# Moving the transposes of the normalised rows ahead of the attention-times-values matmuls

## The chip, the cores and the metric

The kernel runs on all 8 cores of one Trainium2 chip. Each core does the same program on its own 2048 tokens (plus a window of 128 on either side). The metric is the device time in microseconds of the slowest core.

## The reference

```python
def _L0_attn_ref(x, w_qkv):            # x (2, 8192, 1024), 16 heads of 64, windows of 128
    q, k, v = jnp.split(x @ w_qkv, 3, axis=-1)
    ...                                # keys of the window before, the own one, the one after
    scores = einsum('bhnqe,bhnke->bhnqk', q * scale, k_ctx)
    scores = where(valid, scores, NEG)
    out = einsum('bhnqk,bhnke->bhnqe', softmax(scores), v_ctx)

x = layernorm(x + _L0_attn_ref(x, w_qkv))
x = layernorm(x + _L0_ffn_ref(x, ...)) # 8 experts, top 2, d_ff 4096, gelu, all experts computed
```

## The kernel before

One core works in three stages. First it computes q, k and v for its tokens. Then comes attention, window by window, with the first layernorm; its result is kept transposed in x1T. Then come the experts: 32 units, each 512 matmuls with 512 columns.

The instructions of every engine are put in an order written out by hand: helpers (MM for PE, DV for DVE, AC for ACT, SY for SP's queue) append to one list for each engine, with the semaphores that an instruction waits for. An engine works through its list in order. All matmuls have the line of a helper (L151), so they are told apart by tile.

The attention stage is one loop over 256 steps g (L616). A step is a head h of a window w. Windows go in pairs, and the steps alternate between the two windows of a pair: 32 steps a pair, 8 pairs. So an even g belongs to the first window of the pair and an odd g to the second. Iteration g issues, in this order:

- st_nm_exp(g): the row maximum of the scores on DVE (L399) and the exponential on ACT (L407). For the very first and the very last window a mask is added on DVE ahead of it (L391).
- plan_scores(g + 3): the scores matmul (ps_sc) of three steps ahead. There are three score banks, so it waits for the exponential of g.
- st_tr(g): three transposes of the probabilities on PE into one of two banks, ps_pt, by the parity of g.
- st_recip(g - 2): a reciprocal on DVE (L467).
- st_evpt(g - 1): the copy of the transposed probabilities out of ps_pt into probsT (three slots). For an even step it is on DVE (L435), so it is DVE work of the odd iterations; for an odd step it is on ACT (L430).
- st_av(g - 1): three matmuls, probabilities times values (ps_av).
- Up to three evacuations of ps_av on DVE (L477) while some are pending. After the last head of a window follow the residual sum (plan_stt, L492) and the sum of squares on ACT (L511, and L514 on DVE); the rest of the statistics (plan_tail_stats2, L520, L523, L526 on DVE, L530 and L533 on ACT) comes in a later iteration and the normalisation (plan_tail_stats3, L539 and L547 on DVE, which writes x1tmp) in a later one still. That is done by a countdown of 2 and 4 iterations in pend_work.
- The transposed result. For each window gen_tail_mm_pieces makes two pieces. A piece is four transposes of x1tmp on PE into the ps_pt bank of parity g + 1, and one DVE copy of 512 columns into x1T (L570 in the first piece, p12, L586 in the second, p34). Pieces are put in pend_tmpiece once the window is normalised, and each iteration issues at most one, at its end. Windows of the last pair get theirs after the loop.

A ps_pt bank is free for the next transposes when the copy that last read it is done, be it L435, L430, L570 or L586.

Of the kernel before, what the change touches and what calls it, by code (L numbers as in the profile page):

```python
# [85 lines left out]
def build_nc(debug=False):  # L86
# [62 lines left out]
    def MM(dst, lhsT, rhs, start, stop, waits=(), inc=None):  # L149
        fn = (lambda _d, _l, _r, _s, _e:  # L150
              lambda t: t.matmul(_d, _l, _r, start=_s, stop=_e))(dst, lhsT, rhs, start, stop)  # L151
        return p.op("tensor", fn, waits=waits, inc=inc)

    def DV(fn, waits=(), inc=None, drain=True):
        r = p.op("vector", fn, waits=waits, inc=inc)
        if drain:
            p.op("vector", lambda v: v.drain())  # L157
        return r

    def AC(fn, waits=(), inc=None):  # L160
        return p.op("scalar", fn, waits=waits, inc=inc)

    def SY(fn, waits=(), inc=None, n=16):
        w = list(waits)
        if inc is not None:
            w.append((inc, p.val[inc]))
        return p.op("sync", fn, waits=w, inc=inc, n=n)
# [179 lines left out]
    def avbank(w, h):  # L347
        return (4 * (w // 2) + (2 if h >= 8 else 0) + (w % 2)) % 3
# [24 lines left out]
    def plan_scores(g):  # L373
        w, h = steps[g]
        bi = g % 3
        scb[g] = bi
        hp, hb = h // 2, (h % 2) * 64
        w_ = list(bk_sc[bi].rw())
        if g < 2:
            w_ += [(s_ac, qkv_ac_end)]  # L380
        sc_v[g] = MM(ps_sc[bi][:],
                     q_b[hb:hb + 64, hp, 128 * w:128 * (w + 1)],
                     k_b[hb:hb + 64, hp, 128 * w:128 * w + 384],
                     start=True, stop=True, waits=w_, inc=s_mm)

    def st_nm_exp(g):
        w, h = steps[g]
        bi = scb[g]
        bp = g % 3
        if w in (0, NCH - 1):  # L390
            mv = DV((lambda _b: lambda v: v.tensor_tensor(  # L391
                out=ps_sc[_b][:], in0=ps_sc[_b][:], in1=mask_s0[:], op=ALU.add))(bi),
                waits=[(s_mm, sc_v[g]), (s_x, mask_state["v"])], inc=s_dv, drain=True)
            if w == 0 and h == H - 1:
                mask_state["reload"] = mv
        nmw = [(s_mm, sc_v[g])]
        if g - 3 in exp_v:
            nmw.append((s_ac, exp_v[g - 3]))
        nmv = DV((lambda _bi, _bp: lambda v: v.reduce_max(out=stc(C_NM + _bp), in_=ps_sc[_bi][:],  # L399
                                                          axis=AX.X, negate=True))(bi, bp),  # L400
                 waits=nmw, inc=s_dv, drain=False)
        ew = [(s_dv, nmv)]
        if g - 3 in tr_v:
            ew.append((s_mm, tr_v[g - 3]))
        if (w - 2, h) in recip_v:
            ew.append((s_dv, recip_v[(w - 2, h)]))
        exp_v[g] = AC((lambda _bi, _bp, _s: lambda s: s.activation(  # L407
            out=probs_u[:, _bp, :], in_=ps_sc[_bi][:], func=AF.Exp,
            bias=stc(C_NM + _bp), scale=1.0, accum_out=stc(C_L + _s)))(bi, bp, lri(w, h)),
            waits=ew, inc=s_ac)  # L410
        bk_sc[bi].release = [(s_ac, exp_v[g])]

    def st_tr(g):
        bp = g % 3
        bt = g % 2
        for c in range(3):
            w_ = [(s_ac, exp_v[g])] + (bk_pt[bt].rw() if c == 0 else [])
            tr_v[g] = MM(ps_pt[bt][:, 128 * c:128 * (c + 1)],
                         probs_u[:, bp, 128 * c:128 * (c + 1)], I_b[:],
                         start=(c == 0), stop=(c == 2), waits=w_,  # L420
                         inc=(s_mm if c == 2 else None))

    def st_evpt(g):
        bt = g % 2
        sl = g % 3
        epw = [(s_mm, tr_v[g])]
        if g - 3 in av_v:
            epw.append((s_mm, av_v[g - 3]))
        if g % 2 == 1:
            ev = AC((lambda _b, _s: lambda s: s.copy(out=probsT[:, _s, :], in_=ps_pt[_b][:, 0:384]))(bt, sl),  # L430
                    waits=epw, inc=s_ac)
            bk_pt[bt].release = [(s_ac, ev)]
            evpt_v[g] = ("ac", ev)
        else:
            ev = DV((lambda _b, _s: lambda v: v.tensor_copy(out=probsT[:, _s, :], in_=ps_pt[_b][:, 0:384]))(bt, sl),  # L435
                    waits=epw, inc=s_dv, drain=False)
            bk_pt[bt].release = [(s_dv, ev)]
            evpt_v[g] = ("dv", ev)

    def st_av(g):  # L440
        w, h = steps[g]
        sl = g % 3
        aw = avbank(w, h)
        kind, ev = evpt_v[g]
        evw = (s_ac, ev) if kind == "ac" else (s_dv, ev)
        if h % 8 == 0:
            ug = 4 * (w // 2) + (2 if h >= 8 else 0) + (w % 2) - 3
            if ug >= 0:
                tw = 2 * (ug // 4) + (ug % 2)
                th = 7 if (ug % 4) < 2 else 15  # L450
                force_drain(lambda: (tw, th) in evac_v)
        for c in range(3):
            w_ = [evw]
            if h % 8 == 0 and c == 0:
                w_ += bk_av[aw].rw()
            av_v[g] = MM(ps_av[aw][:, 64 * (h % 8):64 * (h % 8) + 64],
                         probsT[:, sl, 128 * c:128 * (c + 1)], v_b[:, w + c, 64 * h:64 * h + 64],
                         start=(h % 8 == 0 and c == 0), stop=(h % 8 == 7 and c == 2),
                         waits=w_, inc=(s_mm if c == 2 else None))
        avg_by_wh[(w, h)] = av_v[g]  # L460

    def st_recip(g):
        w, h = steps[g]
        rw_ = [(s_ac, exp_v[g])]
        if (w - 2, h) in evac_v:
            rw_.append((s_dv, evac_v[(w - 2, h)]))
        recip_v[(w, h)] = DV((lambda _s: lambda v: v.reciprocal(  # L467
            out=stc(C_RI + _s), in_=stc(C_L + _s)))(lri(w, h)),
            waits=rw_, inc=s_dv, drain=False)
# [130 lines left out]
    pend_tmpiece = []  # L600
    pend_work = []

    def force_drain(cond):
        while not cond():
            we, he = pend_evac.pop(0)
            plan_evac(we, he)
            if he == 15:
                plan_stt(we)
                plan_tail_stats1(we)
                pend_work.append([2, (lambda _w: lambda: plan_tail_stats2(_w))(we)])  # L610
                pend_work.append([4, (lambda _w: lambda: plan_tail_stats3(_w))(we)])
# [4 lines left out]
    for g in range(NST):  # L616
        w, h = steps[g]
        st_nm_exp(g)
        if g + 3 < NST:
            plan_scores(g + 3)  # L620
        st_tr(g)
        if g >= 2:
            st_recip(g - 2)
        if g >= 1:
            st_evpt(g - 1)
            st_av(g - 1)
            wp, hp_ = steps[g - 1]
            if hp_ == 7:
                pend_evac += [(wp, hh) for hh in range(8)]
            if hp_ == 15:  # L630
                pend_evac += [(wp, hh) for hh in range(8, 16)]
        if mask_state["reload"] is not None and not mask_state.get("reloaded"):
            mask_state["v"] = SY(lambda e: e.dma_start(out=mask_s0[:], in_=mrd),
                                 waits=[(s_dv, mask_state["reload"])], inc=s_x)
            mask_state["reloaded"] = True
        n_done = 0
        while pend_evac and n_done < 3:
            we, he = pend_evac[0]
            if (we, he) not in recip_v:
                break  # L640
            plan_evac(we, he)
            pend_evac.pop(0)
            n_done += 1
            if he == 15:
                plan_stt(we)
                plan_tail_stats1(we)
                pend_work.append([2, (lambda _w: lambda: plan_tail_stats2(_w))(we)])
                pend_work.append([4, (lambda _w: lambda: plan_tail_stats3(_w))(we)])
        for item in pend_work:
            item[0] -= 1  # L650
        while pend_work and pend_work[0][0] <= 0:
            pend_work.pop(0)[1]()
        if h == 0 and w % 2 == 0 and w >= 2:
            pend_tailmm += [w - 2, w - 1]
        while pend_tailmm and pend_tailmm[0] in x1ap_v:
            pend_tmpiece += gen_tail_mm_pieces(pend_tailmm.pop(0))
        if pend_tmpiece:
            pend_tmpiece.pop(0)((g + 1) % 2)
    st_evpt(NST - 1)
    st_av(NST - 1)  # L660
    wlast, hlast = steps[NST - 1]
# [332 lines left out]
```

How the kernel before makes its waits and increments, by code:

```python
            def body(eng_obj):  # L59
                for waits, fn, inc, n in self.streams[name]:
                    for (s, v) in waits:
                        eng_obj.wait_ge(s, v)
                    bi = fn(eng_obj)
                    if inc is not None:
                        bi.then_inc(inc, n)
```

## Time and profile before

| | us |
|---|---|
| median of 3 runs | 4558.41 |
| lowest run | 4555.35 |
| profiled execution | 4560.75 |
| its span (slowest core) | 4558.3 |
| span of the fastest core | 4539.9 |

The profile is of one execution, on the slowest core (core 5). PE is TensorE, PEld its weight loads, DVE VectorE, ACT ScalarE. In the timeline a row has the start in us from the start of the span, the duration in us, the engine, the line, the operation, what it writes and reads, the shapes and the count, and in brackets how long the engine had been idle ahead of it and what ended the wait. The attention stage lies between about 350 and 864 us of the span, and the experts fill the rest of it.

### The profile page before, as it was taken

Reading aid. Unit: us, or ns where it says so; the run is one execution under the profiler, and the core shown is the slowest. Engines: PE = TensorE matmul, PEld = TensorE weight load, DVE = VectorE, ACT = ScalarE, POOL = GpSimd, SP = SyncE. Lnnn points to the kernel's source line nnn. Section 1 sums busy time; section 2 is a strip of 40 time slices with the busy share of each in tenths; the row PEclk is TensorE's granted clock in tenths of the full one; section 3 lists DMA queues with packets and bytes.
Section 4 is the critical chain, followed back from the end, with each engine's and each line's share of the span. In section 5 each row is a group of like instructions: output and inputs, shape, how many; then the busy total and the mean of one; then the engine's idle time right before and its main releaser. Section 6 shows DMA issues by size and latency. Waiting matters only on the chain.

```text
span 4558.3 us, 48557 instructions; the slowest of 8 cores (4539.9 to 4558.3 us)
## 1 busy us (share of the span) xinstructions
PE 4108.2 (90%) x19776; PEld 1912.6 (42%) x19776; DVE 1141.1 (25%) x1978; ACT 902.2 (20%) x1415; POOL 76.8 (2%) x92
## 2 busy tenths in 40 slices
PE   5865555479999999999999999999999999999995
PEld 3333333234444444444444444444444444444442
DVE  1016666631111111111111111111111111111126
ACT  1224444211111111111111111111111111111111
POOL 0000000000000000000000000000000000000000
PEclk9885555579999999999999999999999999999997
DMA  6652000012222222222222222222222222222211
GB/s 115 100 86 48 19 19 19 1 19 38 38 37 37 37 38 37 37 37 38 37 38 42 43 44 39 38 37 37 37 37 38 37 37 37 38 37 38 43 32 74
DMA packets 97483, 187.26 MB, mean 41 GB/s; under 512 B 3426, under 2 KB 24290, under 8 KB 97258
## 3 DMA queue, kind: packets, MB, share of 16 engines
q0 software_dynamic: 89616, 157.36, 21.5%
q1 hardware_dynamic: 7650, 26.81, 1.7%
q8 instruction: 161, 2.64, 0.2%
q14 instruction: 56, 0.46, 0.0%
HBM read 333.12 MB, written 8.39 MB: 75 GB/s over the span
## 4 chain that ended last, share of the span: by engine, by line
PE 86%; DVE 6%; issue 3%; DMA 2%; ACT 1%; DVEq 1%; ACTq 0%; SPq 0%; POOLq 0%
PE ps_y L151 39%; PE ps_h L151 39%; PE ps_qk L151 4%; PE ps_pt L151 2%; DVE stats L399 2%; PE ps_sc L151 2%; DMA W1g<-wqkv 1%; DMA xch_q<-xh 1%; ACT probs_u L407 1%; DVEq L157 1%; DVE attn_sb L477 1%; DVE xpre L492 0%; DVE y_acc L787 0%; DVE outb L855 0%; DVE probsT L435 0%
## 5 line engine op out<-in xcount | busy, mean ns | idle before, releaser
L151 PE MATMUL ps_h<-x1T,W1g 128*128 128x512 bf16 x8192 | 1778.0, 380 | 36.0 <-ACT hpr L888 36.0
L151 PE MATMUL ps_y<-W2g,hpr 128*128 128x512 bf16 x8192 | 1783.4, 380 | 0.4 <-DVE y_acc L787 0.4
L913 DVE SCALAR_TENSOR_TENSOR y_acc<-ps_y,wgt,y_acc 128x1024 f32<-128x1024 f32 x512 | 657.1, 1283 | 2811.5 <-PE ps_y L151 2810.8
L151 PEld LDWEIGHTS ps_h<-x1T,W1g 128*128 128x128 bf16 x8192 | 802.6, 98 | 1006.0 <-issue 42.7
L151 PEld LDWEIGHTS ps_y<-W2g,hpr 128*128 128x128 bf16 x8192 | 803.2, 98 | 971.9 <-issue 12.6
L888 ACT ACTIVATE hpr<-ps_h,b1T 128x1024 bf16<-128x1024 f32 x512 | 570.4, 1114 | 2945.3 <-PE ps_h L151 2945.3
L151 PE MATMUL ps_sc<-k_b,q_b 64*128 64x384 bf16 x256 | 122.3, 480 | 217.5 <-ACT probs_u L407 214.7
L407 ACT ACTIVATE probs_u<-ps_sc,stats 128x384 bf16<-128x384 f32 x256 | 149.5, 584 | 253.6 <-DVE stats L467 245.9
L151 PE MATMUL ps_qk<-xT_S,W1g 128*128 128x512 bf16 (+3 forms) x640 | 140.3, 389 | 45.2 <-DMA W1g<-wqkv 31.2
L399 DVE TENSOR_REDUCE stats<-ps_sc 128x1 f32<-128x384 f32 x256 | 138.8, 545 | 2.9
L151 PEld LDWEIGHTS ps_sc<-k_b,q_b 64*128 64x128 bf16 x256 | 25.7, 101 | 251.2 <-issue 244.6
L151 PE MATMUL ps_pt<-I_b,probs_u 128*128 128x128 bf16 x768 | 128.5, 305 | 1.5 <-ACT probs_u L407 1.4
L151 PEld LDWEIGHTS ps_qk<-xT_S,W1g 128*128 128x128 bf16 x640 | 66.7, 110 | 117.9 <-issue 70.8
L435 DVE CAST probsT<-ps_pt 128x384 bf16<-128x384 f32 x128 | 71.1, 556 | 121.5 <-PE ps_pt L151 119.0
L151 PEld LDWEIGHTS ps_pt<-I_b,probs_u 128*128 128x128 bf16 x768 | 61.2, 125 | 85.8 <-issue 85.8
L151 PE MATMUL ps_av<-v_b,probsT 128*128 128x64 bf16 x768 | 93.9, 248 | 0.7 <-ACT probsT L430 0.6
L151 PEld LDWEIGHTS ps_av<-v_b,probsT 128*128 128x128 bf16 x768 | 74.8, 141 | 3.1 <-issue 1.5
L248 DVE CAST xT_S<-ps_tr 128x512 bf16<-128x512 f32 x18 | 12.4, 692 | 217.0 <-PE ps_tr L151 217.0
L893 POOL DMA_DIRECT2D W1g<-w x31 | 27.1, 874 | 2268.5 <-PE ps_h L151 1630.0
L151 PE MATMUL ps_qk<-W2g,xT_S 128*128 128x512 bf16 x288 | 63.1, 379 | 0.0
L430 ACT CAST probsT<-ps_pt 128x384 bf16<-128x384 f32 x128 | 60.1, 470 | 1.8 <-PE ps_pt L151 1.8
L477 DVE TENSOR_SCALAR attn_sb<-ps_av,stats 128x64 bf16<-128x64 f32 x256 | 57.1, 274 | 11.2 <-PE ps_av L151 11.0
(89 smaller groups left out, 664.2 us busy)
## 6 DMA issues: line engine op xcount, KB each, us to landing
W1g<-w POOLq DMA_DIRECT2D x32, 2048.0 KB, 15.7
W2g<-w POOLq DMA_DIRECT2D x32, 2048.0 KB, 15.7
W1g<-wqkv POOLq DMA_DIRECT2D x20, 1024.0 KB, 11.0
xch_q<-xh SPq DMA_DIRECT2D x18, 512.0 KB
xch<-xh SPq DMA_DIRECT2D x16, 512.0 KB
out<-outb SPq DMA_DIRECT2D x16, 512.0 KB, 2.6
W2g<-wqkv POOLq DMA_DIRECT2D x1, 2048.0 KB, 20.6
mask_s<-maskl SPq DMA_DIRECT2D x1, 192.0 KB
```

The costliest lines, as they stand in the source:

```text
L151: lambda t: t.matmul(_d, _l, _r, start=_s, stop=_e))(dst, lhsT, rhs, start, stop)
L157: p.op("vector", lambda v: v.drain())
L248: DV((lambda _jr, _bk, _sp: lambda v: v.tensor_copy(out=xT_S[:, _sp, 0:4, _jr:_jr + 128], in_=_bk.ap[:, 0:512]))(jr, bank, sp), waits=evw, ...
L399: nmv = DV((lambda _bi, _bp: lambda v: v.reduce_max(out=stc(C_NM + _bp), in_=ps_sc[_bi][:], axis=AX.X, negate=True))(bi, bp), waits=nmw, i ...
L407: exp_v[g] = AC((lambda _bi, _bp, _s: lambda s: s.activation(out=probs_u[:, _bp, :], in_=ps_sc[_bi][:], func=AF.Exp, bias=stc(C_NM + _bp), ...
L430: ev = AC((lambda _b, _s: lambda s: s.copy(out=probsT[:, _s, :], in_=ps_pt[_b][:, 0:384]))(bt, sl), waits=epw, inc=s_ac)
L435: ev = DV((lambda _b, _s: lambda v: v.tensor_copy(out=probsT[:, _s, :], in_=ps_pt[_b][:, 0:384]))(bt, sl), waits=epw, inc=s_dv, drain=False)
L477: evac_v[(w, h)] = DV((lambda _w, _h, _aw, _s: lambda v: v.tensor_scalar(out=attn_sb[:, _w % 2, 64 * _h:64 * _h + 64], in0=ps_av[_aw][:, 6 ...
L888: gel_pr[pr] = AC((lambda _fc, _pr, _bk, _col: lambda s: s.activation(out=hpr[:, _fc, 1024 * _pr:1024 * (_pr + 1)], in_=_bk.ap[:], func=AF ...
L893: wld["w1", u + 1] = GP((lambda _u: lambda e_: e_.dma_start(out=W1g[:], in_=w1_ap(_u)))(u + 1), waits=[(s_mm, hend)], inc=s_w) if u + 1 < ...
L913: ev = DV((lambda _tq, _pp, _e: lambda v: v.scalar_tensor_tensor(out=y_acc[:, _tq, :], in0=ps_y[_pp][:], scalar=wgt[:, _tq, _e:_e + 1], in ...
```

## The change

The statement that issues a pending piece is moved inside the iteration, from its end to the place between st_evpt(g - 1) and st_av(g - 1). The argument, by which the bank is chosen, stays the same. The pieces are still put in pend_tmpiece at the end of an iteration, so a new piece is issued in the following iteration at the earliest.

```diff
@@ -623,6 +623,8 @@
             st_recip(g - 2)
         if g >= 1:
             st_evpt(g - 1)
+            if pend_tmpiece:
+                pend_tmpiece.pop(0)((g + 1) % 2)
             st_av(g - 1)
             wp, hp_ = steps[g - 1]
             if hp_ == 7:
@@ -654,8 +656,6 @@
             pend_tailmm += [w - 2, w - 1]
         while pend_tailmm and pend_tailmm[0] in x1ap_v:
             pend_tmpiece += gen_tail_mm_pieces(pend_tailmm.pop(0))
-        if pend_tmpiece:
-            pend_tmpiece.pop(0)((g + 1) % 2)
     st_evpt(NST - 1)
```

## Rows read from the trace of the kernel before

**Rows 1.** Busy time by stretch: stretch, length, each engine, granted clock, DMA share, GB/s

```profile
400.00:465.00 65.00, 36.15 (x245) 20.75 (x243) 41.22 (x134) 29.51 (x88) 0.00 (x0) 0.50 0.05 17
2000.00:2500.00 500.00, 500.00 (x2319) 226.68 (x2317) 101.83 (x80) 72.42 (x65) 7.87 (x9) 1.00 0.23 38
```

**Rows 2.** List of cores: span and granted clock of the shortest and the longest

```profile
core 2: 4539.9 us, clock 0.922
...
core 5: 4558.3 us, clock 0.919
```

**Rows 3.** Timeline, steps 6 to 12 of a pair, the chain of two steps

```profile
414.25 0.55 DVE L399 TENSOR_REDUCE stats<-ps_sc 128x1 f32<-128x384 f32 x1
...
414.89 0.58 ACT L407 ACTIVATE probs_u<-ps_sc,stats 128x384 bf16<-128x384 f32 x1 [2.06 <-DVE stats L467]
...
415.71 0.47 PE L151 MATMUL ps_sc<-k_b,q_b 64*128 64x384 bf16 x1 [2.17 <-ACT probs_u L407]
...
416.11 0.50 PE L151 MATMUL ps_pt<-I_b,probs_u 128*128 128x128 bf16 x3
...
416.41 0.37 PE L151 MATMUL ps_av<-v_b,probsT 128*128 128x64 bf16 x3
...
416.72 0.56 DVE L435 CAST probsT<-ps_pt 128x384 bf16<-128x384 f32 x1 [1.33 <-PE ps_pt L151]
...
426.90 0.56 DVE L435 CAST probsT<-ps_pt 128x384 bf16<-128x384 f32 x1 [1.37 <-PE ps_pt L151]
...
427.37 0.55 DVE L399 TENSOR_REDUCE stats<-ps_sc 128x1 f32<-128x384 f32 x1
```

**Rows 4.** Instructions on tile x1T: what ended DVE's idle time before them

```profile
  PE ps_pt L151: 38.9, 29
```

**Rows 5.** Timeline of the same pair, iterations 4 and 5

```profile
408.33 0.81 DVE L547 TENSOR_SCALAR x1tmp<-xpre,stats 128x1024 bf16<-128x1024 f32 x1
...
409.98 0.69 DVE L570 CAST x1T<-ps_pt 128x512 bf16<-128x512 f32 x1 [0.83 <-PE ps_pt L151]
410.58 0.55 DVE L399 TENSOR_REDUCE stats<-ps_sc 128x1 f32<-128x384 f32 x1
...
411.12 0.54 DVE L435 CAST probsT<-ps_pt 128x384 bf16<-128x384 f32 x1
...
411.57 0.14 DVE L520 TENSOR_SCALAR stats<-stats 128x1 f32<-128x1 f32 x1
...
412.44 0.50 PE L151 MATMUL ps_pt<-I_b,probs_u 128*128 128x128 bf16 x3
...
412.92 0.61 PE L151 MATMUL ps_pt<-I_b,x1tmp 128*128 128x128 bf16 x4
413.64 0.69 DVE L586 CAST x1T<-ps_pt 128x512 bf16<-128x512 f32 x1 [1.40 <-PE ps_pt L151]
```

**Rows 6.** Timeline of the same pair, iterations 7 and 8

```profile
417.48 0.81 DVE L547 TENSOR_SCALAR x1tmp<-xpre,stats 128x1024 bf16<-128x1024 f32 x1
...
419.74 0.55 DVE L399 TENSOR_REDUCE stats<-ps_sc 128x1 f32<-128x384 f32 x1
...
422.80 0.69 DVE L586 CAST x1T<-ps_pt 128x512 bf16<-128x512 f32 x1 [2.44 <-PE ps_pt L151]
```

**Rows 7.** Timeline of the same pair: statistics, and a wait after a drain

```profile
403.12 0.14 DVE L520 TENSOR_SCALAR stats<-stats 128x1 f32<-128x1 f32 x1
...
403.71 0.55 DVE L399 TENSOR_REDUCE stats<-ps_sc 128x1 f32<-128x384 f32 x1
...
407.93 0.15 DVE L514 TENSOR_SCALAR stats<-stats 128x1 f32<-128x1 f32 x1 [0.16 <-DVE xpre L492]
```

**Rows 8.** Timeline of the last pair, with the mask in odd steps

```profile
793.90 0.81 DVE L547 TENSOR_SCALAR x1tmp<-xpre,stats 128x1024 bf16<-128x1024 f32 x1
...
796.15 0.56 DVE L391 TENSOR_TENSOR ps_sc<-ps_sc,mask_s 128x384 f32<-128x384 f32 x1
796.80 0.56 DVE L399 TENSOR_REDUCE stats<-ps_sc 128x1 f32<-128x384 f32 x1
...
813.79 0.56 DVE L435 CAST probsT<-ps_pt 128x384 bf16<-128x384 f32 x1 [0.71 <-PE ps_pt L151]
```

## Prediction

> **What bounds the kernel now.** I read the page first, for which engine is full where. Over the whole span PE is busy, but a table of two stretches splits that in two [rows 1]: in the expert layers (2000 to 2500 us) PE is busy for all 500 us at a granted clock of 1.00, while in the attention stretch where the change lies (400 to 465 us, one pair of windows) PE is busy for 36.15 of 65 us, DVE for 41.22, ACT for 29.51, at a clock of 0.50 (1.2 GHz). No engine is full there, so the stretch is set by a chain through several of them, and the expert layers, which begin after it, are simply shifted by whatever the attention stretch gains or loses. The list of cores [rows 2] shows how much the whole differs by itself: 4539.9 to 4558.3 us, 18 us or 0.4%.
>
> Then the timeline of one steady piece [rows 3], to see that chain. I write i for the step counted from the first step of the new pair (g = 32k + i). Read in order: the row maximum of step 6 on DVE starts at 414.25; its exponential on ACT at 414.89 (+0.64 to 0.65); the scores matmul of step 9, which needs the bank that this exponential read, at 415.71 (+0.82); the transposes of step 6 at 416.11 (+0.40); the value matmuls of step 5 at 416.41 (+0.30); the DVE copy of step 6's transposed probabilities (L435) at 416.72 (transposes + 0.61). That copy belongs to iteration 7. The next even maximum follows a copy by 0.47 (426.90 to 427.37). So two steps cost 0.65 + 0.82 + 0.40 + 0.61 + 0.47 = 2.95 us when nothing is in the way, and DVE idles 1.33 us of it, waiting for PE in the *odd* iteration, at L435. This is the key to placing work on DVE: in an even iteration it can fill that idle time; in an odd one, behind L435, it adds its whole length.
>
> **Where the pieces stand now.** A piece is four transposes of x1tmp on PE and one DVE copy to x1T. A pair makes four: p12 and p34 of its first window (w), then p12' and p34' of the second (w+1). There are 32 copies (two lines, 16 each), 28 of them made inside the loop, four for each of seven pairs. Before them DVE sits idle 38.9 us in all waiting for PE [rows 4]. From the counts in the code (three evacuations per iteration, statistics 2 and 4 iterations later) the iterations are now: p12 at 4, p34 at 5, p12' at 7, p34' at 8, each at the end. The rows agree [rows 5, 6]:
> p12 follows the normalisation L547 (408.33, 0.81 long) directly. PE has long finished its own work, so DVE waits only 0.83 and copies at 409.98; the next maximum is at 410.58 (copy + 0.60).
> p34, iteration 5: the maximum 410.58, L435 at 411.12, the three statistics L520 to L526 from 411.57 in the shadow of the wait, transposes of the step at 412.44, the piece's at 412.92 behind the value matmuls, the copy at 413.64, the next maximum at 414.25.
> p12', iteration 7: like p12, behind L547 of 417.48; the maximum of step 8 at 419.74.
> p34', iteration 8: the copy at 422.80 after 2.44 us idle, so the maximum of step 9 is at 422.80 + 0.60 = 423.40. The next odd-iteration L435 (step 10, when all four pieces are done) is at 426.90 [rows 3]: this is the point at which I compare.
>
> **The change part by part.** No instruction is added or removed. A piece generated at the end of an iteration is now popped one iteration later, between the copy of the probabilities of step g-1 and the value matmuls of g-1. So the iterations become 5, 6, 8, 9. The bank is the same one ((g+1) % 2 = (g-1) % 2), freed by the copy just ahead of it in the code, which the value matmuls waited for anyway: no new wait on PE from that. Two things move, though. On PE the piece stands ahead of three value matmuls, so it starts 0.30 after the transposes instead of 0.48 (412.44 to 412.92): 0.18 earlier. On DVE its copy stands ahead of the evacuations and statistics of the iteration, and behind the wait it needs: maximum of g, exponential of g, scores, transposes of g, piece. That is 0.65 + 0.82 + 0.40 + 0.30 + 0.72 (412.92 to 413.64) = 2.89 us after the maximum of the same iteration; with 0.60 for the copy the following work starts 3.49 us after it. DVE has only 0.54 to 1.0 us of work to put under that.
>
> Forward from L547's end at 409.14. A drain costs 0.16 [rows 7].
> Iteration 5: maximum at 409.30 (1.28 earlier than now). L435 at 409.84, hidden. Piece p12 copied at 409.30 + 2.89 = 412.19; statistics at 412.79, now uncovered; the next maximum is 0.59 after L520 (403.12 to 403.71) [rows 7]: 413.38. Now it is 414.25, so the lead has shrunk to 0.87, with one piece owed.
> Iteration 6: maximum of 7 at 413.38 + 3.49 = 416.87. Its L435 follows at once (416.87 + 0.54 = 417.41, against 416.72 now), L539 0.47 later, L547 0.29 behind that, at 418.17, end 418.98, maximum of 8 at 419.14 (now 419.74): lead 0.60.
> Iteration 8: maximum of 9 at 419.14 + 3.49 = 422.63 (now 423.40): lead 0.77, p34' still owed.
> Iteration 9: maximum of 10 at 422.63 + 3.49 = 426.12. Then the bare chain, 0.65 + 0.82 + 0.40 + 0.61 = 2.48, to L435 of step 10: 428.60. Now it is 426.90. Loss of the pair: **1.70 us**.
>
> Said as costs: today p12 and p12' cost 1.28 each, as they find PE idle, p34 about 2.1 and p34' about 1.7. Moved, none finds PE idle: two stand in even iterations, where the 1.33 us of slack takes part of the 3.49 (about 1.5 each), two in odd ones (about 2.5 each). 8.1 against 6.4.
>
> Six pairs show the same intervals, the L570 and L586 idle times to 0.01 us. In the seventh the odd steps add a mask on DVE (L391, 0.65 from it to the maximum) [rows 8]. Same working: L547 ends 794.71, mask 794.87, maximum 795.52, copy 798.41, next maximum 799.60, copy of p34 802.49, mask 803.09, maximum 803.74, L435 804.28, L547 805.04 to 805.85, maximum of 8 806.01, copy 808.90, mask 809.50, maximum of 9 810.15, maximum of 10 813.64, L435 816.12, against 813.79 now: 2.33. In all 6 × 1.70 + 2.33 = 12.5 us. The profiled execution took 4560.75 us at a span of 4558.3; the median of the runs is 4558.41. So 4558.41 + 12.5 = 4571 us, slower by 0.27%.
>
> What is costed at nothing: the value matmuls come about 0.45 us later in 28 iterations. The copy that reuses their probsT slot comes three steps later, and the scores matmul queued behind them waits for an exponential that starts later still. If that cover were missing, each would add up to 0.45: 13 us. No DMA is moved and no queue other than PE's and DVE's.
>
> That a piece can't be done earlier rests on PE's order. The row of p34 shows it: its operands and bank were there once L435 of 411.12 had ended (411.66), and its matmuls started at 412.92, behind transposes and value matmuls [rows 5]. The Trainium skill says the same ("TensorE: Matmul & The Clock Gate", Part 2, step by step): TensorE pulls only weight loads ahead, and the matmuls stay in program order. By that rule the 1.70 stands; were it otherwise, a piece would cost DVE its bare 0.60.
>
> **The rivals.** (a) The change does not matter: the shift of 13 us is swallowed. For it speaks that the cores alone differ by 18 us and that only 28 of 256 iterations are touched; against it, that the chain has no outside clock in this stretch to be late for. Time 4558, give or take 5.
> (b) Faster: the pieces leave the tail of L547, where DVE pays 0.83 us of pure waiting, and are covered where they go. The point that decides is whether PE has the transposes ready when DVE arrives at the copy. If it did in all 28, a pair would cost 4 × 0.60 = 2.4 instead of 6.4: 28 us less, 4530; if only in the two even iterations, where DVE idles anyway, 2 × 1.5 - 1.70 = 1.3 us gained a pair, about 4549. Against it is the chain of rows 3: transposes of g can't start before 1.87 us after the maximum of g.
> (c) Slower than forecast: the late value matmuls do hold the next scores (the 13 us above), or the copy of an odd iteration holds more than I see. 4571 + 13 = 4584.
> (d) TensorE's clock. It is granted 0.50 in the stretch, with PE busy 36.15 of 65 us [rows 1]. If denser work raised it to 1.00, scores-to-transposes and transposes-to-copy would shrink by up to half of 0.40 + 0.61, 0.5 us in 2.95, over 128 double steps 65 us: 4505. The Trainium skill's same page (Part 1) holds that sustained activity raises the clock and idleness keeps it low; here PE's gaps get longer, not shorter, so the trace gives it no ground. In the other direction the expert layers at a lower clock would cost over 2% whatever the change does.
>
> **How the numbers follow.** Forecast 0.72, (a) 0.13, (b) 0.05, (c) 0.08, (d) 0.02 in both directions. The predicted time is 4571. The forecast by itself allows 8 to 18 us (a third off in either term of 8.1 and 6.4 apart) and some 4 us for the executions, 4562 to 4581. The range for 8 in 10 takes in (a)'s middle and (c): 4554 to 4588. About 2% (91 us) is what counts as a difference; it would need 3 us a piece, more than any row offers. Faster 0.01, same 0.97, slower 0.02.
>
> **What would show it.** In the changed kernel, the copies L570 and L586 of the pair should each stand 2.89 us behind the maximum of their iteration, with idle times before them of about 1.8 (odd) and 2.3 us (even), 8.2 a pair where now it is 5.5; L547 should be followed by a maximum after 0.16 without a wait; L435 of iteration 7 should have no wait (now 1.33); the pair should be 1.7 us longer and the attention stretch end about 12.5 us later. It is wrong if the copies are found earlier than 2.89 behind the maximum, if the scores matmul behind the value matmuls has a new wait, or if the clock of the stretch is not 0.50.

## The result

The change makes the kernel slower by about 11 us, a quarter of a per cent: the ratio of the times is 1.0024, with a 95% interval of 1.0012 to 1.0036. In a second comparison (e10 below) it was 1.0027, 1.0016 to 1.0037. Differences under 2% count as "same", so by that bound it is the same.

| | before | changed |
|---|---|---|
| ratio | 1 | 1.0024 |
| lowest execution | 4554.94 | 4565.52 |
| profiled execution | 4560.75 | 4568.37 |
| median of all executions | 4622.64 (17) | 4774.71 (13) |

In 7 of these 13 executions of the changed kernel, and by their times in about half of the 17 of the kernel before, the four cores of one die ran at a lower granted clock (down to 0.78 instead of 0.92) and took up to 730 us longer, so the median of all is mostly these, and the ratio leaves them out.

**The profile after.** The busy time of the two stretches, the same view as [rows 1]. The clock is 0.50 and 1.00 as before, and DVE is busy less of the attention stretch:

```profile
400.00:465.00 65.00, 35.52 (x240) 20.89 (x240) 39.88 (x131) 28.87 (x88) 0.00 (x0) 0.50 0.04 16
2000.00:2500.00 500.00, 497.58 (x2272) 226.67 (x2317) 98.83 (x77) 75.75 (x68) 7.87 (x9) 1.00 0.21 38
```

The timeline of the first pair (columns as in the rows of before), iterations 5 to 10. This answers to [rows 5, 6]:

```profile
405.18 0.81 DVE L547 TENSOR_SCALAR x1tmp<-xpre,stats 128x1024 bf16<-128x1024 f32 x1
...
406.09 0.56 DVE L399 TENSOR_REDUCE stats<-ps_sc 128x1 f32<-128x384 f32 x1
...
406.63 0.54 DVE L435 CAST probsT<-ps_pt 128x384 bf16<-128x384 f32 x1
...
407.96 0.50 PE L151 MATMUL ps_pt<-I_b,probs_u 128*128 128x128 bf16 x3
408.26 0.63 PE L151 MATMUL ps_pt<-I_b,x1tmp 128*128 128x128 bf16 x4
408.68 0.36 PE L151 MATMUL ps_av<-v_b,probsT 128*128 128x64 bf16 x3
408.99 0.69 DVE L570 CAST x1T<-ps_pt 128x512 bf16<-128x512 f32 x1 [1.82 <-PE ps_pt L151]
409.60 0.14 DVE L520 TENSOR_SCALAR stats<-stats 128x1 f32<-128x1 f32 x1
...
410.19 0.55 DVE L399 TENSOR_REDUCE stats<-ps_sc 128x1 f32<-128x384 f32 x1
...
413.08 0.69 DVE L586 CAST x1T<-ps_pt 128x512 bf16<-128x512 f32 x1 [2.28 <-PE ps_pt L151]
413.69 0.55 DVE L399 TENSOR_REDUCE stats<-ps_sc 128x1 f32<-128x384 f32 x1
...
414.23 0.54 DVE L435 CAST probsT<-ps_pt 128x384 bf16<-128x384 f32 x1
...
414.96 0.81 DVE L547 TENSOR_SCALAR x1tmp<-xpre,stats 128x1024 bf16<-128x1024 f32 x1
...
418.77 0.69 DVE L570 CAST x1T<-ps_pt 128x512 bf16<-128x512 f32 x1 [2.28 <-PE ps_pt L151]
...
422.28 0.69 DVE L586 CAST x1T<-ps_pt 128x512 bf16<-128x512 f32 x1 [1.83 <-PE ps_pt L151]
...
425.36 0.56 DVE L435 CAST probsT<-ps_pt 128x384 bf16<-128x384 f32 x1 [1.33 <-PE ps_pt L151]
```

Read it from the row maximum down. It starts at 406.09, and the copy of the piece at 408.99, 2.90 later; at 410.19 and 413.08, 2.89. Between them TensorE works off its list: the transposes of the step, then the piece (the value matmuls come behind it). DVE stands for 1.82 and 2.28 us. From the first L547 to the L435 of step 10 it is 425.36 - 405.18 = 20.18 us, against 426.90 - 408.33 = 18.57 before: 1.61 a pair. L435 of iteration 7 (414.23) no longer waits, since the piece ahead of it has used its waiting time.

DVE's idle time ahead of all 32 copies, the view of [rows 4], went from 38.9 us to this:

```profile
  PE ps_pt L151: 58.0, 29
```

Now the whole. The profiled core is another one than before, so I compare distances in one core. I use two through the document: **six periods**, from the first L547 of the first pair to that of the seventh, and **the rest**, from there to the first matmul of the gating, which ends the attention stage. After, these are the rows (the first of the seven L547 stands above):

```profile
800.62 0.81 DVE L547 TENSOR_SCALAR x1tmp<-xpre,stats 128x1024 bf16<-128x1024 f32 x1
...
873.06 2.27 PE L151 MATMUL ps_y<-bg_s,ones_f 1*128 1x8 f32 x10 [1.05 <-DVE x1T L586]
```

and before, with [rows 5, 8] for the two L547, the gating starts here:

```profile
864.08 2.27 PE L151 MATMUL ps_y<-bg_s,ones_f 1*128 1x8 f32 x10 [1.05 <-DVE x1T L586]
```

Six periods are 800.62 - 405.18 = 395.44, before 793.90 - 408.33 = 385.57: +9.87, 1.64 a period. The rest is 72.44 against 70.18: +2.26. Together 12.1 us, all in the stretch where the pieces are. From the gating to the end of the span it is 4566.8 - 873.06 = 3693.7, before 4558.3 - 864.08 = 3694.2: within 0.5 us nothing is given back there and nothing added. The two spans themselves differ by only 8.5 us because in this execution the first L547 happened to stand 3.15 us earlier (405.18 against 408.33).

### The profile page after: what moved, and what is told of

Read it like the earlier page. It is cut to its first block, busy times and chain, and to the rows that moved or that the text cites. A ratio compares the mean times of both kernels' runs of the same rounds, so it can differ in the third digit from the quotient of the medians.

```text
span 4566.8 us, 48210 instructions; the slowest of 8 cores (4554.6 to 4566.8 us)
## 1 busy us (share of the span) xinstructions
PE 4087.8 (90%) x19429; PEld 1916.2 (42%) x19776; DVE 1141.7 (25%) x1978; ACT 901.2 (20%) x1415; POOL 76.6 (2%) x92
## 4 chain that ended last, share of the span: by engine, by line
PE 85%; DVE 7%; issue 4%; DMA 2%; ACT 1%; DVEq 1%; ACTq 0%; SPq 0%; POOLq 0%
PE ps_y L151 39%; PE ps_h L151 38%; PE ps_qk L151 4%; PE ps_pt L151 2%; DVE stats L399 2%; PE ps_sc L151 2%; DMA W1g<-wqkv 1%; ACT probs_u L407 1%; DMA xch_q<-xh 1%; DVEq L157 1%; DVE attn_sb L477 1%; DVE xpre L492 0%; DVE probsT L435 0%; DVE y_acc L787 0%; DVE outb L855 0%
## 5 line engine op out<-in xcount | busy, mean ns | idle before, releaser
L435 DVE CAST probsT<-ps_pt 128x384 bf16<-128x384 f32 x128 | 70.9, 554 | 112.6 <-PE ps_pt L151 110.0
```

## The experiments

The attention stage repeats within 0.25 us: over the eight cores of one execution six periods take 385.53 to 385.75 in the kernel before and 395.41 to 395.57 in the changed one (395.57 in e10, another execution). So the two distances tell a few tenths of a microsecond apart, where the kernel's time can't. The rows of e1 to e8 are of core 0. All kernels:

| kernel | pieces in iterations | six periods | the rest | sum against before |
|---|---|---|---|---|
| before | 4, 5, 7, 8 (end) | 385.57 | 70.18 | 0 |
| changed | 5, 6, 8, 9 | 395.44 | 72.44 | +12.1 |
| e1 delay only | 5, 6, 8, 9 (end) | 395.67 | 72.53 | +12.5 |
| e2 place only | 4 (end), 5, 7 (end), 8 | 387.45 | 70.47 | +2.2 |
| e3 even only | 6, 8, 10, 12 | 384.81 | 72.04 | +1.1 |
| e4 odd only | 5, 7, 9, 11 | 390.50 | 70.78 | +5.5 |
| e5 no pieces | none | 346.23 | 63.23 | -46.3 |
| e6 copy later on DVE | as e3 | 372.58 | 67.47 | -15.7 |
| e7 copy later on ACT | as e3 | 346.22 | 61.97 | -47.6 |
| e8 copy later on ACT | as changed | 350.20 | 62.91 | -42.6 |

**e1: the delay without the place.**

```diff
+        if pend_tmpiece:
+            pend_tmpiece.pop(0)((g + 1) % 2)
         while pend_tailmm and pend_tailmm[0] in x1ap_v:
             pend_tmpiece += gen_tail_mm_pieces(pend_tailmm.pop(0))
-        if pend_tmpiece:
-            pend_tmpiece.pop(0)((g + 1) % 2)
```

> The change is two edits in one: a piece comes one iteration later, and it stands ahead of the value matmuls. This kernel does the first alone: pieces at the end of iterations 5, 6, 8 and 9 of a pair. Theory (the delay does the harm, as DVE then meets TensorE before the step's own transposes are done, the place hardly matters): the copies stand 3.07 us behind the row maximum of their iteration in even iterations, and a pair becomes 1.8 us longer than before, against 1.6 in the changed kernel; six pair periods sum to 396.5 us (before 385.57, changed 395.44), all in all +12 to +13 us. Rival (the place ahead of the value matmuls does the harm): six periods stay within 2 us of 385.57 and the time that of before.

Measured: six periods 395.67 (expected 396.5), +12.5 us in all in the trace. The ratio of the times, 1.0020 (0.9995 to 1.0045), does not by itself exclude 1. The delay alone does it all. The place gives back 0.2 us of it over six periods, a difference as small as the spread. That is not because the place does nothing, but because it does two things that nearly cancel. Iteration 5 of e1 (core 0):

```profile
395.04 0.56 DVE L399 TENSOR_REDUCE stats<-ps_sc 128x1 f32<-128x384 f32 x1
...
396.04 0.15 DVE L520 TENSOR_SCALAR stats<-stats 128x1 f32<-128x1 f32 x1
...
398.11 0.69 DVE L570 CAST x1T<-ps_pt 128x512 bf16<-128x512 f32 x1 [1.39 <-PE ps_pt L151]
398.72 0.55 DVE L399 TENSOR_REDUCE stats<-ps_sc 128x1 f32<-128x384 f32 x1
```

The copy stands 3.07 us behind the maximum, where in the changed kernel it is 2.90: the place brings each of the four copies of a pair about 0.17 us nearer to its maximum. But here the statistics (L520) run inside the wait, and in the changed kernel they stand uncovered behind the copy. So in iteration 5 the next maximum follows after 3.68 us here and after 4.10 there (406.09 to 410.19), 0.42 more, against 3 × 0.17 less in the other three.

**e2: the place without the delay.**

```diff
+            if pend_tmpiece:
+                pend_tmpiece.pop(0)((g + 1) % 2)   # between st_evpt(g - 1) and st_av(g - 1)
...
-        if pend_tmpiece:
+        if len(pend_tmpiece) % 2 == 0 and pend_tmpiece:
             pend_tmpiece.pop(0)((g + 1) % 2)       # at the end of the iteration
```

> The place alone, without the delay: the first piece of a window at the end of iterations 4 and 7 as before, the second ahead of the value matmuls of iterations 5 and 8. Theory (the delay does the harm): +0.4 us in iteration 5, whose statistics now stand behind the copy instead of in its shadow, -0.2 in iteration 8, +0.2 us a pair, so six periods sum to about 387 us, whole kernel +1.6 us. Rival (the place does the harm): half the loss of the change, 0.8 us a pair, 390.5.

Measured: six periods 387.45 (expected about 387, rival 390.5), +1.9; the sum is +2.2. It stands near the theory's 1.6 and far from the half of the change. Here the place is worth 0.31 a pair against, not for: the same 0.42 of uncovered statistics in iteration 5, and only one other piece (iteration 8) that gains its 0.17, which makes 0.25. So the effects of the two edits do not simply add. Between e1 and e2 the loss is assigned to the delay: the first piece of a window used to be issued right behind its normalisation, at a moment when TensorE had nothing else to do. One iteration later it is queued behind that iteration's exponential, scores and transposes.

**e3 and e4: which iterations.** Both take the changed kernel and let a piece out in every second iteration only.

```diff
-            if pend_tmpiece:
+            if pend_tmpiece and g % 2 == 0:        # e4: g % 2 == 1
                 pend_tmpiece.pop(0)((g + 1) % 2)
```

> As the changed kernel, but pieces are let out in even iterations only (6, 8, 10, 12 of a pair), where no DVE copy of probabilities stands in the way. Theory (a piece costs 1.55 us in an even iteration, as it takes 1.33 us of idle DVE time for its own, and 2.5 in an odd one behind other DVE work): a pair 0.2 us shorter than before, six periods 384.5 us, whole kernel -1 to -2 us. Rival (any piece behind the row maximum of its iteration costs the same 2 us): 8 us a pair as in the changed kernel, six periods 395.

> The same with odd iterations only (5, 7, 9, 11). Theory, worked out step by step: the first costs 2.5 us as in the changed kernel, the others, which follow an even iteration without a piece, 1.56 each, so that a pair is about 0.8 us longer than before, six periods 390.4 us, whole kernel +5. Rival (an odd iteration costs 2.5 always): 10 against 6.4, +3.6 a pair, six periods 407.

Measured: six periods 384.81 (expected 384.5) and 390.50 (expected 390.4). So the price of a piece is set by what else waits in its pair of iterations. The timeline of e4 shows the cheap kind of odd piece, in iterations 6 and 7 (core 0):

```profile
409.52 0.55 DVE L399 TENSOR_REDUCE stats<-ps_sc 128x1 f32<-128x384 f32 x1
...
410.06 0.54 DVE L399 TENSOR_REDUCE stats<-ps_sc 128x1 f32<-128x384 f32 x1
...
412.00 0.56 DVE L435 CAST probsT<-ps_pt 128x384 bf16<-128x384 f32 x1 [1.33 <-PE ps_pt L151]
413.45 0.69 DVE L586 CAST x1T<-ps_pt 128x512 bf16<-128x512 f32 x1 [0.90 <-PE ps_pt L151]
```

The two row maxima stand next to each other, so the transposes of both steps are under way at once. L435 takes its usual 1.33 us wait and the piece adds only 0.90, where in iteration 9 of the changed kernel (the copy at 422.28) it is 1.83. There the maximum of the odd step comes late, held by the piece of the even one.

These two also show that idle time ahead of an instruction is not its price. In e4 the idle time ahead of all copies is less than before:

```profile
  PE ps_pt L151: 32.3, 29
```

32.3 against the 38.9 of [rows 4], and the kernel is slower by 5.5 us. In e3 it is 65.1, more than in the changed kernel, and the loss is 1.1.

One part of the expectation of e3 failed: the whole was to be 1 to 2 us shorter and is 1.1 longer, by the rest, 1.9 us up. It lies in the seventh pair, from its first L547 (790.64) to that of the eighth (851.61), 60.97 against 59.11 before (793.90 to 853.01). There a mask is added in odd steps (core 0):

```profile
796.68 0.69 DVE L570 CAST x1T<-ps_pt 128x512 bf16<-128x512 f32 x1 [2.29 <-PE ps_pt L151]
797.29 0.56 DVE L391 TENSOR_TENSOR ps_sc<-ps_sc,mask_s 128x384 f32<-128x384 f32 x1
797.94 0.56 DVE L399 TENSOR_REDUCE stats<-ps_sc 128x1 f32<-128x384 f32 x1
```

L391 and the maximum of the odd step used to run inside the even step's wait, which shrank from 1.33 to 0.71 us by it [rows 8]. So a piece in an even iteration has 0.65 us less idle time to use up. e3 has three more such pieces in this pair than the kernel before: 3 × 0.65 - 0.13, the gain of an ordinary pair, is 1.8 us, near the 1.9 measured. The mask as the cause is a reading of these rows and was not tested by itself.

**e5: no pieces.** The loop drops its pieces; x1T is set to zero at the start.

```diff
-        if pend_tmpiece:
-            pend_tmpiece.pop(0)((g + 1) % 2)
+        pend_tmpiece.clear()
```

> Leaves out the 28 pieces of the loop (transposes and copies of windows 0 to 13; x1T is set to zero at the start instead), so it gives what the pieces cost in all. By the step-by-step working the pieces of a pair cost 6.4 us in the kernel before and 8.0 in the changed one: six periods sum to 385.57 - 38.4 = 347.2 us. Rival (pieces are mostly covered by idle DVE time and the loss in the changed kernel has another source): six periods within 12 us of 385.57, that is not under 373.

Measured: six periods 346.23, expected 347.2. So the pieces cost (385.57 - 346.23) / 6 = 6.56 us a pair before and (395.44 - 346.23) / 6 = 8.20 in the changed kernel. The change in itself is small beside what the pieces cost in either place.

**e6, e7, e8: who waits.** The piece is split: its transposes are issued ahead of the value matmuls of g, its copy in iteration g + 1 behind the maximum and the exponential. In e6 the copy stays on DVE.

```diff
         st_nm_exp(g)
+        if pend_copy:
+            pend_copy.pop(0)()
...
+            if pend_tmpiece and g % 2 == 0:        # e8: without the condition on g
+                pend_copy.append(pend_tmpiece.pop(0)((g + 1) % 2))
             st_av(g - 1)
...
-            cast = DV((lambda _j, _b: lambda v: v.tensor_copy(   # e7, e8, in both pieces
-                out=x1T[:, 0:4, ...], in_=ps_pt[_b][:, 0:512]))(j, bank), ...
+            cast = AC((lambda _j, _b: lambda s: s.copy(
+                out=x1T[:, 0:4, ...], in_=ps_pt[_b][:, 0:512].rearrange(...)))(j, bank), ...
```

> Transposes ahead of the value matmuls in even iterations as in e3, but the DVE copy is put one iteration later, behind the next row maximum. Theory (what costs is that DVE stands waiting for the transposes with the next row maximum behind it): that maximum is no longer held, the copy still waits till 2.89 us after the even maximum and holds the copy of probabilities by 1.0 us instead of 1.55: 4 us a pair against 6.4, six periods 371. Rival (the bank, held one copy longer, delays the next step's transposes and gives it back): no shorter than e3, 384.

> As e6, with the copy on ACT behind the next exponential. Theory (DVE's wait is all there is to a piece's cost): DVE has nothing to do with the piece, ACT waits in time it has idle, and the next transposes have 0.7 us of room: pieces cost under 1 us a pair, six periods 347 to 353, whole kernel 38 to 45 us faster than before. Rival (the chain through ACT is held instead, next exponential behind the waiting copy): 0.9 us a piece, 3.6 a pair, six periods 369, whole kernel 18 us faster.

> As e7, but in the iterations of the changed kernel (5, 6, 8, 9), each piece ahead of the value matmuls. If DVE's wait is the whole of the loss and neither the delay nor the place matter without it, this kernel is within 6 us of e7: six periods under 359. If the delay or the place cost by themselves through TensorE's order, it keeps the changed kernel's 1.6 us a pair and more over e7 (six periods over 360).

Measured: 372.58 (expected 371), 346.22 (347 to 353, so 0.8 below the range) and 350.20 (under 359). In e6 the copy is still on DVE but no longer ahead of the next maximum, and the pieces cost (372.58 - 346.23) / 6 = 4.4 us a pair. e7 is where e5 is, within the spread: with the copy on ACT the pieces are done and cost the attention loop nothing. So all 6.56 us a pair was DVE waiting and copying with the next work of the chain behind it. In the rest e7 is even 1.3 us shorter than e5. Of that 1.1 lies behind the last normalisation, where e5 still copies the last pieces on DVE: from there to the gating it is 4.04 us in e5 (801.74 to 805.78, core 0) and 2.95 in e9, the repetition of e7 (816.46 to 819.41). This is also why e7 gains more in all (47.6 us) than the 38 to 45 expected. e8, in the changed kernel's iterations, keeps 0.66 us a pair over e7. It differs from e7 in the closer spacing and in the use of odd iterations, and no run tells the two apart.

A piece of the kernel of e7, as its repetition e9 shows it (iterations 6 and 7):

```profile
415.49 0.50 PE L151 MATMUL ps_pt<-I_b,probs_u 128*128 128x128 bf16 x3
...
415.78 0.63 PE L151 MATMUL ps_pt<-I_b,x1tmp 128*128 128x128 bf16 x4
416.10 0.56 DVE L435 CAST probsT<-ps_pt 128x384 bf16<-128x384 f32 x1 [1.33 <-PE ps_pt L151]
...
416.51 0.59 ACT L571 CAST x1T<-ps_pt 128x512 bf16<-128x512 f32 x1 [0.63 <-PE ps_pt L151]
...
417.24 0.48 PE L151 MATMUL ps_pt<-I_b,probs_u 128*128 128x128 bf16 x3 [0.23 <-ACT x1T L571]
```

TensorE does the piece at 415.78 while DVE goes on with L435 at its usual time. ACT waits 0.63 us in time that it has idle. The bank is held one copy longer, so the next transposes wait 0.23 us for it: the rival of e6 is visible in that row, and as six periods of e7 are those of e5, it costs nothing.

**e9 and e10: the two times side by side.**

> The kernel of e7 again, now for its time. Its trace has the attention stretch shorter by 39.4 us over six pair periods and by 8.2 from there to the gating matmuls, 47.6 us in all; if nothing is given back in the expert layers, the time is 4558.4 - 47.6 = 4511 us, ratio 0.9896. Rival (the expert layers, which are bound by TensorE, take some of it back): ratio above 0.993.

> The changed kernel again, on the same chip as e9. Its trace has 9.9 us over six pair periods and 2.3 from there to the gating matmuls, 12.1 in all: 4570.5 us, ratio 1.0027. Rival (the slowest core's own spread hides it): interval of the ratio takes in 1.000.

Measured: e9 has a ratio of 0.9891 (0.9871 to 0.9911), expected 0.9896; the two shortest of its five executions, on which the ratio rests, took 4511.48 and 4516.0 us. e10 has 1.0027 (1.0016 to 1.0037), expected 1.0027. Their distances were 346.30 and 61.99, and 395.57 and 72.49. So the version that takes the copies off DVE is 1.1% faster than the kernel before, and by the two ratios (0.9891 / 1.0027) 1.4% faster than the changed one. Under the 2% bound that too counts as same; it is four times the size of the change.

## Why the prediction was right and wrong

**The chain of two steps** was right, and what was computed from it came out within 0.1 us a piece: the copies 2.90 and 2.89 us behind the maximum of their iteration (forecast 2.89), idle times of 1.82 and 2.28 (about 1.8 and 2.3), L435 of iteration 7 without a wait. The order on TensorE, on which it rests, held in the row of 408.26: by that rule of the Trainium skill ("TensorE: Matmul & The Clock Gate", Part 2), the piece can't overtake the step's transposes, and the trace agrees, as it starts 0.30 us behind them though x1tmp had been complete since 405.99 and the bank free since L435 ended at 407.17.

**The sum.** The forecast was 6 × 1.70 + 2.33 = 12.5 us, the trace has 9.87 + 2.26 = 12.1. A small term that was off is the drain behind L547: I took 0.16 us for it from the row of L514, but the maximum follows at 406.09 - 405.18 = 0.91 where I had 0.97. It is 0.06 less, twice a pair, so 0.12; the first pair came out only 0.09 under the forecast and the six on average 0.06, so other small terms went the other way. One of these is known by its place: in the fourth pair the copy of iteration 6 waits 2.48 us instead of 2.28 and the period is 1.80 longer than before, not 1.6. Why is open.

**The costs of a piece**, 6.4 us a pair before and 8.1 after, were measured by e5: 6.56 and 8.20. Both were 0.1 to 0.2 short, and that cancels in their difference. The prices of 1.5 for an even and 2.5 for an odd iteration were right for these places and are not general: in e4 the pieces of a pair cost (390.50 - 346.23) / 6 = 7.4 us, which after 2.5 for the first leaves 1.6 for each of the other three odd pieces, with no even piece ahead of them.

**What was named as the change.** I treated the delay and the place together. The delay was the whole of the loss (e1). The place was worth almost nothing, as the 0.18 us that the forecast had for TensorE's order, 0.17 by e1, is spent again on the statistics that lose their cover in iteration 5 (e1, e2). The forecast had both terms in its steps but did not set them against each other.

**Costed at nothing** were the value matmuls that come 0.42 us later (408.26 to 408.68). No wait appeared behind them, and e7, which has them just as late in its even iterations and is as fast as e5, settles it for those. For the odd ones e1 speaks: it has them at the old place in the same iterations and is no faster. Rival (c) falls with it. Rival (b), that the pieces would be covered, falls with the direction of the result, and by e3: even in even iterations alone there is only 0.8 us to gain over six periods (expected 1.1), since TensorE has not got the transposes ready when DVE arrives. Rival (a) falls by the two intervals that leave out 1.000. Rival (d): the clock stayed at 0.50, also in e9, where TensorE is busy 38.79 of 65 us.

**What was wrong** is the range. 4554 to 4588 holds the six shortest of the changed kernel's 13 executions (4565.52 to 4568.81) and not the median of all, 4774.71. The step that failed is the last term of the range, "some 4 us for the executions". What the runs showed in its place is a scatter of 734 us, 4565.52 to 5299.26. It does not come from the change, since the kernel before scatters as much (4554.94 to 5232.38), and why an execution falls on the long side no run here tells. It could have been allowed for: one of the three times of before was already 4805.12, some 250 us above the other two, and I took no account of it. The way and the size of the change were right: 12.5 forecast, 12.1 in the trace, a ratio that makes 10.9 us (5.5 to 16.4). The point value of 4571 is 2 to 5 us above the six shortest executions.

One more step of the range does not follow, though it did no harm: a third off in either of the terms 8.1 and 6.4 would be 2.7 or 2.1 us a pair, 15 to 19 us over seven pairs, and not the 4 to 6 us that "8 to 18" allows.

## What to carry over

Before moving an instruction of an in-order engine, ask when its operands will be there by the other engine's list at the new place, not at the old one. Here, right behind the normalisation, TensorE is idle and a round trip with its copy costs about 1.3 us by the prediction's working; one iteration later it costs 1.5 to 2.5. And where such a round trip recurs, it was worth more to let an engine with idle time do the waiting (6.6 us a pair, e7) than to find the best place on the engine that carries the chain (0.13 us a pair, e3).

## What was not expected of the hardware

Copying 128x512 f32 out of PSUM took 586 ns on ACT (L571) and 692 on DVE (L570), so the engine with the free time is also the quicker one for this copy. And the attention stage, set by round trips between three engines, repeats within 0.25 us in 386 from core to core, while the same cores' whole spans differ by 18 us.
